# Bias products of a routed expert layer behind the expert loop, and nine expert weight loads issued by GpSimd two at a time

## The chip, the cores and the metric

One core of one Trainium2 chip. The metric is the device time of one execution in microseconds. TensorE is called PE, its weight loads PEld, VectorE DVE, ScalarE ACT, GpSimd POOL and SyncE SP, as in the profile. A "q" behind a name (SPq, ACTq) is that engine's sequencer, which issues DMAs.

## What is computed

`x` has 1250 rows of 512. It is normalized, goes through a graph layer (neighbour sums over 40,000 edges, then two matrix products with 1024 hidden columns) and an attention layer with 8 heads, and both results are added to `x`. The sum goes through a layer of 16 experts, of which each row uses two. Only this last part matters here:

```python
xt = layernorm(x)                                   # 1250 x 512
probs = softmax(xt @ router_w.T + router_b)         # 1250 x 16
topk_p, topk_i = top_k(probs, 2)
gates = sum(one_hot(topk_i) * topk_p[..., None], axis=1)      # 1250 x 16, two nonzero per row
for each expert e:
    h = gelu(xt @ w1[e].T + b1[e])                  # 256 hidden
    y = h @ w2[e].T + b2[e]                         # 512
    out += y * gates[:, e]
result = x + out
```

The sum over experts of gate times second bias is the product `gates @ b2` (1250 x 16 by 16 x 512), which the kernel computes by itself. It is called the bias product below.

## The kernel before

The 1250 rows are ten tiles of 128 (the last has 98). Each engine has its own program, and semaphores order them. The residual sum lies in SBUF as `xr`, tile by tile. An engine works through its program in order: an instruction behind a wait does not start before the wait is over.

**The graph layer's second half and the routing** run over the groups of tiles `FC_TILES` (0 to 2, 3 to 5, 6 and 7, 8 and 9). PE computes the hidden columns (L1234) and the second product (L1180), DVE adds it to `xr` (L948) and normalizes, PE turns the normalized rows and computes router logits (L1198), DVE picks the two best experts of each row, and PE counts how many earlier rows chose the same expert (L1205). DVE then knows for each row two slots in a DRAM buffer `slots`, sorted by expert (`place`). POOL scatters each tile's rows there, twice, with indirect DMAs (L552, 20 in all, semaphore `scattered`). After the last group DVE works out which expert each tile of slots belongs to and how many pairs of tiles there are, signals `route_ready` (L982), and computes the last gates (`weigh`, L983, semaphore `gates_ready`).

**The weights of the 16 experts** are 1 MB each (128 partitions of 8 KB, w1 and w2 together) and all fit in SBUF once the earlier parts are done. Each load is one DMA with a semaphore of its own, `ew_in[e]`. SP issues experts 0 and 15 (L376) while the graph layer runs, 9, 10 and 11 (L380) when its hidden columns are done, and 12, 13 and 14 (L391) just ahead of its part of the expert loop. ACT issues experts 1 to 8 (L668) when the graph layer's last product is done (`mix_ps`). POOL, after its last scatter, waits for the loads in the order of the experts and counts them into one semaphore, `w_ready` (L556 to L558), which DVE and PE compare with a number read at run time.

**The bias products** stand between routing and expert loop. For each tile PE turns its gates (L1265, into PSUM bank 0 or 1), ACT copies them out (L673, `gt_saved`), PE multiplies by `b2` (L1271, into bank 2 or 3), and DVE adds the result to `xr` (L988, `gb_added`). With two banks for each, PE's product of tile t waits for DVE's add of tile t - 2.

**The expert loop** takes two tiles of slots a turn. SP waits for `route_ready` and for all scatters, and fetches the first two tiles (L385, `xg_in`); PE turns them (`turn_rows`, L1277), ACT copies (L677), and SP fetches the next two (L388). DVE's `take_w1` (L994 to L998) waits for `w_ready` of the tile's expert and copies its w1 to a fixed place; PE's first product (L1295) needs that copy. ACT applies gelu (L687), PE turns the next rows and multiplies by w2 (L1308), DVE copies the result out (L1010), and SP stores it into `slots` (L400).

**The end.** When all results are stored, POOL gathers for each tile of rows the two results (L568, 20 indirect DMAs), DVE multiplies each by its gate and adds it to `xr` (L1015, L1017), and SP stores the tile (L405).

The order in which POOL counts, and what DVE waits for:

```python
for e in range(EXP):                      # POOL, L556
    pool.wait_ge(ew_in[e], 16)
    pool.sem_inc(w_ready, 1)
...
dve.wait_ge(w_ready, e + 1)               # DVE, take_w1, L997
dve.tensor_copy(w1_now[:, a, :], arena[:, bass.ds(lies, KD * DFF)]).then_inc(w1_ready[a], 1)
```

Of the kernel before, what the change touches and what calls it, by code (L numbers as in the profile page):

```python
# [23 lines left out]
P = 128  # L24
N = 1250
D = 512
NT = 10
# [6 lines left out]
FC_TILES = [range(0, 3), range(3, 6), range(6, 8), range(8, 10)]  # L34
# [18 lines left out]
EXP = 16  # L53
DFF = 256
KF = DFF // P
EW = KD * DFF + KF * D
# [10 lines left out]
def layer(nc, x, src, dst, wqkv, wo, bo, gw1, gb1, gw2, gb2, geps, rw, rb, ew, eb1, eb2, out):  # L67
    f32r = mybir.dt.float32r
    f32, f16, bf16, i32 = mybir.dt.float32, mybir.dt.float16, mybir.dt.bfloat16, mybir.dt.int32
    ALU = mybir.AluOpType  # L70
# [5 lines left out]
    with ExitStack() as ctx:  # L76
# [10 lines left out]
        arena = sb("arena", [P, SLAB // 4])  # L87
# [75 lines left out]
        xr = at(VT + NT * D * 4, [NT, D])  # L163
# [29 lines left out]
        ident = sb("ident", [P, P])  # L193
# [95 lines left out]
        def rows(t):  # L289
            return LAST if t == NT - 1 else P  # L290
# [45 lines left out]
        def _(sp):  # L336
# [25 lines left out]
            def expert(e):  # L362
                sp.dma_start(arena[:, expert_at(e):expert_at(e) + EW], ew[e]).then_inc(ew_in[e], 16)
# [23 lines left out]
                sp.wait_ge(xgt_ps[a], 1)  # L387
                sp.dma_start(xg[:, a, :], rows_of(2 + a)).then_inc(xg_in[a], 16)  # L388

            for e in (12, 13, 14):  # L390
                expert(e)  # L391
            n = sp.value_load(npair[0:1, 0:1], min_val=1, max_val=(MAXT - 3) // 2)
            with sp.Fori(0, n) as j:
                for a in range(2):
# [14 lines left out]
        def _(pool):  # L409
# [139 lines left out]
            for t in range(NT):  # L549
                pool.wait_ge(slots_ready, 1 + sum(1 for tiles in FC_TILES if tiles[-1] < t))  # L550
                for k in range(2):
                    pool.indirect_dma_start(  # L552
                        out=xs, out_offset=bass.IndirectOffsetOnAxis(ap=slot[0:rows(t), k, t:t + 1], axis=0),
                        in_=x2n[0:rows(t), t, :], in_offset=None).then_inc(scattered, 16)

            for e in range(EXP):  # L556
                pool.wait_ge(ew_in[e], 16)
                pool.sem_inc(w_ready, 1)  # L558
# [15 lines left out]
        def _(act):  # L574
# [89 lines left out]
                    act.activation(x2n_t[:, t % 2, :, :], bank[6][:, :].rearrange("p (k n) -> p k n", k=KD),  # L664
                                   copy).then_inc(x2nt_saved, 1)
            act.wait_ge(mix_ps, NT)
            for e in range(1, 9):
                act.dma_start(arena[:, expert_at(e):expert_at(e) + EW], ew[e]).then_inc(ew_in[e], 16)  # L668
            exponents(len(FC_TILES) - 1)

            for t in range(NT):
                act.wait_ge(gt_ps, t + 1)
                act.activation(gates_t[:, t * P:(t + 1) * P], bank[t % 2][0:EXP, 0:P], copy).then_inc(gt_saved, 1)  # L673

            for a in range(2):
                act.wait_ge(xgt_ps[a], 1)
                act.activation(xg_t[:, a, :, :], bank[4 + a][:, :].rearrange("p (k n) -> p k n", k=KD),  # L677
                               copy).then_inc(xgt_saved[a], 1)
            act.wait_ge(eb1_in, 16)
            act.wait_ge(route_ready, 1)  # L680
            n = act.value_load(npair[0:1, 0:1], min_val=1, max_val=(MAXT - 3) // 2)
# [15 lines left out]
        def _(dve):  # L697
# [284 lines left out]
            dve.sem_inc(route_ready, 1)  # L982
            weigh(len(FC_TILES) - 1)  # L983

            for t in range(NT):
                r = rows(t)
                dve.wait_ge(gb_ps, t + 1)
                dve.tensor_tensor(xr[0:r, t, :], xr[0:r, t, :], bank[2 + t % 2][0:r, :], ALU.add).then_inc(gb_added, 1)  # L988


            for a in range(2):
                dve.sem_inc(y_saved[a], 1)
                dve.sem_inc(y_stored[a], 16)
# [17 lines left out]

            for t in range(NT):
                r = rows(t)
                dve.wait_ge(yg_in[t], 32)
                link(dve.scalar_tensor_tensor(out=xr[0:r, t, :], in0=yg[0:r, 0, t, :], scalar=gate[0:r, 0, t:t + 1],  # L1015
                                              in1=xr[0:r, t, :], op0=ALU.mult, op1=ALU.add))
                dve.scalar_tensor_tensor(out=xr[0:r, t, :], in0=yg[0:r, 1, t, :], scalar=gate[0:r, 1, t:t + 1],  # L1017
                                         in1=xr[0:r, t, :], op0=ALU.mult, op1=ALU.add).then_inc(res_ready, 1)

        @block.tensor  # L1020
        def _(pe):
# [234 lines left out]
            route(NT - 1)  # L1256
            ranks(len(FC_TILES) - 1)

            pe.wait_ge(b2_in, 16)
            for f, tiles in enumerate(FC_TILES):  # L1260
                pe.wait_ge(gates_ready, f + 1)
                for t in tiles:
                    if t >= 2:
                        pe.wait_ge(gt_saved, t - 1)
                    pe.transpose(bank[t % 2][0:EXP, 0:P], gates[:, t, :], ident[:, :]).then_inc(gt_ps, 1)  # L1265
                for t in tiles:
                    r = rows(t)
                    pe.wait_ge(gt_saved, t + 1)
                    if t >= 2:
                        pe.wait_ge(gb_added, t - 1)  # L1270
                    pe.matmul(bank[2 + t % 2][0:r, :], gates_t[:, t * P:t * P + r], b2_sb[:, :],  # L1271
                              start=True, stop=True).then_inc(gb_ps, 1)


            def turn_rows(a):
                for k in range(KD):
                    ins = pe.transpose(bank[4 + a][:, k * P:(k + 1) * P], xg[:, a, k * P:(k + 1) * P], ident[:, :])  # L1277
                ins.then_inc(xgt_ps[a], 1)

            pe.wait_ge(x2_ready, NT)  # L1280
            for a in range(2):
                pe.wait_ge(xg_in[a], 16)
                turn_rows(a)
            pe.wait_ge(route_ready, 1)
            n = pe.value_load(npair[0:1, 0:1], min_val=1, max_val=(MAXT - 3) // 2)
            with pe.Fori(0, n) as j:
# [16 lines left out]
                for a in range(2):  # L1303
                    pe.wait_ge(w_ready, e[a] + 1)
                    pe.wait_ge(hg_ready[a], j + 1)
                    pe.wait_ge(y_saved[a], j + 1)
                    for k in range(KF):
                        ins = pe.matmul(bank[6 + a][:, :], hg_t[:, a, k, :],  # L1308
                                        arena[:, bass.ds(lies[a] + KD * DFF + k * D, D)],
                                        start=(k == 0), stop=(k == KF - 1))  # L1310
                    ins.then_inc(y_ps[a], 1)


# [29 lines left out]
```

## Time and profile before

| | |
|---|---|
| median of 3 runs | 882.88 us (881.28 to 884.25) |
| profiled execution, its own time | 883.28 us |
| its span in the profile | 881.5 us |
| mean granted PE clock | 0.942 |
| PE, DVE, ACT, POOL busy | 773.4, 519.3, 280.9, 154.5 us |

The span runs from the first to the last instruction of the profile. All positions below are microseconds from its start. Busy time of an engine counts neither waits nor the issuing of DMAs, except on POOL, whose DMA issues are listed as its work. The granted clock is a share of the full 2.4 GHz.

### The profile page before, as it was taken

How to read it: one execution, taken by the hardware profiler on the slowest of the kernel's cores; microseconds unless marked ns; L12 is line 12 of the kernel's file. 1: busy time of each engine (PE TensorE's matmuls, PEld its weight loads, DVE VectorE, ACT ScalarE, POOL GpSimd, SP SyncE). 2: the span in 40 equal slices, each digit the busy share in tenths (PEclk: the TensorE clock that was granted, in tenths of full speed). 3: DMA queues.
4: the chain of work that ended last, by engine and by line, in shares of the span. 5: the costliest groups of instructions: out<-in, count | busy, mean ns of one | idle time of the engine just before them, and what ended most of it. 6: DMA issues, size and time to landing. Idle time of an engine off the chain costs nothing.

```text
span 881.5 us, 11457 instructions
## 1 busy us (share of the span) xinstructions
PE 773.4 (88%) x3351; PEld 517.5 (59%) x3352; DVE 519.3 (59%) x1488; ACT 280.9 (32%) x575; POOL 154.5 (18%) x198
## 2 busy tenths in 40 slices
PE   1999998998989998989799999999998599999910
PEld 1555543665756665666577744677887256766700
DVE  6444345797989899888977535434445533333224
ACT  1311111352525443434345401323333123434400
POOL 5040002112040304040400043002021100000044
PEclk9999999998999999989899999999999559999965
DMA  9016000807153435344261081001015945343357
GB/s 301 2 41 242 1 0 1 293 2 237 59 165 131 140 145 160 134 124 172 65 230 48 1 336 67 1 0 63 10 73 191 365 183 197 108 139 111 129 167 229
DMA packets 47015, 111.61 MB, mean 127 GB/s; under 512 B 7034, under 2 KB 7050, under 8 KB 44528
## 3 DMA queue, kind: packets, MB, share of 16 engines
q1 hardware_dynamic: 42192, 91.41, 30.6%
q0 software_dynamic: 3616, 11.17, 4.0%
q10 hardware_dynamic: 1152, 8.39, 2.4%
q8 instruction: 24, 0.39, 0.2%
q14 instruction: 31, 0.25, 0.1%
HBM read 44.73 MB, written 58.54 MB: 117 GB/s over the span
## 4 chain that ended last, share of the span: by engine, by line
PE 72%; DVE 18%; issue 4%; POOL 2%; DMA 2%; ACT 1%; DVEq 0%; POOLq 0%; SPq 0%
PE bank L1082 9%; PE bank L1104 8%; PE bank L1234 7%; PE bank L1180 6%; PE bank L1295 6%; PE bank L1131 6%; PE bank L1308 5%; DVE arena L797 5%; DVE p_lo L833 5%; PE bank L1053 4%; PE bank L1114 4%; PE bank L1165 4%; PE bank L1150 4%; PE bank L1147 3%; DVE arena L799 3%
## 5 line engine op out<-in xcount | busy, mean ns | idle before, releaser
L630 ACT ACTIVATE p_hi<-bank 128x416 fp32r<-128x416 f32 (+1 forms) x240 | 124.0, 519 | 201.6 <-PE bank L1131 200.2
L833 DVE SCALAR_TENSOR_TENSOR p_lo<-bank,p_hi 128x416 fp32r<-128x416 f32 (+1 forms) x240 | 140.2, 586 | 40.8 <-ACT p_hi L630 39.7
L797 DVE TENSOR_SCALAR arena<-iota,arena 125x128 f16<-125x128 f16 x392 | 135.5, 346 | 42.0 <-PE bank L1053 39.8
L799 DVE TENSOR_SCALAR arena<-iota,arena 125x320 f16<-125x320 f16 x392 | 115.8, 295 | 0.0
L1131 PE MATMUL bank<-q_hi,k_hl 128*128 128x416 f32 (+1 forms) x240 | 114.6, 478 | 0.1
L1150 PE MATMUL bank<-p_lo,v_hl 128*128 128x416 f32 (+1 forms) x240 | 90.8, 378 | 22.4 <-DVE p_lo L833 22.0
L1082 PE MATMUL bank<-arena 128*128 128x512 f32 x200 | 103.9, 601 | 0.8 <-ACT arena L597 0.8
L1053 PE MATMUL bank<-arena 125*128 125x320 f16 x392 | 95.8, 309 | 5.1 <-issue 4.0
L1147 PE MATMUL bank<-p_hi,v_hl 128*128 128x416 f32 (+1 forms) x240 | 86.5, 360 | 0.0
L1131 PE MATMUL bank<-q_lo,k_hl 128*128 128x416 f32 (+1 forms) x240 | 86.1, 359 | 0.0
L1053 PEld LDWEIGHTS bank<-arena 125*128 125x128 f16 x392 | 34.4, 99 | 74.5 <-issue 53.8
L1104 PE MATMUL bank<-arena 128*128 128x416 f32 (+1 forms) x192 | 70.1, 513 | 0.8 <-ACT arena L582 0.8
L1234 PE MATMUL bank<-arena 128*128 128x384 f32 (+2 forms) x256 | 70.3, 430 | 0.0
L1150 PEld LDWEIGHTS bank<-p_lo,v_hl 128*128 128x128 f32 x240 | 46.4, 193 | 36.4 <-DVE p_lo L833 35.1
L1295 PEld LDWEIGHTS bank<-arena 128*128 128x128 f32 x448 | 52.8, 197 | 17.2 <-issue 15.8
L1295 PE MATMUL bank<-arena 128*128 128x128 f32 x448 | 55.1, 283 | 6.4 <-issue 5.4
L998 DVE COPY arena<-arena 128x1024 f32 x30 | 20.8, 695 | 66.9 <-issue 66.9
L1131 PEld LDWEIGHTS bank<-q_hi,k_hl 128*128 128x128 f32 x240 | 47.0, 196 | 20.2 <-issue 13.5
L1234 PEld LDWEIGHTS bank<-arena 128*128 128x128 f32 x256 | 47.7, 190 | 17.6 <-issue 0.5
L492 POOL COPY arena<-arena 125x20 f32 (+1 forms) x40 | 8.6, 214 | 249.7 <-DVE arena L799 213.7
L1104 PEld LDWEIGHTS bank<-arena 128*128 128x128 f32 x192 | 35.2, 189 | 27.1 <-issue 26.5
L1308 PE MATMUL bank<-arena 128*128 x112 | 50.4, 592 | 0.0
(208 smaller groups left out, 1019.4 us busy)
## 6 DMA issues: line engine op xcount, KB each, us to landing
slots<-arena SPq DMA_DIRECT2D x6, 5376.0 KB, 19.1
slots<-arena SPq DMA_DIRECT2D x2, 5120.0 KB, 19.1
arena<-in_ew SPq DMA_DIRECT2D x8, 1024.0 KB, 10.2
arena<-in_ew ACTq DMA_DIRECT2D x8, 1024.0 KB, 12.9
arena<-slots SPq DMA_DIRECT2D x32, 256.0 KB, 2.8
slots<-arena SPq DMA_DIRECT2D x28, 256.0 KB, 2.0
arena<-in_gw SPq DMA_DIRECT2D x2, 2048.0 KB, 17.0
arena<-in_wqkv SPq DMA_DIRECT2D x4, 768.0 KB, 16.5
```

Of the source, the lines that this page charges most:

```text
L630: act.activation(p_hi[0:kt, s % NPB, 0:n], bank[s % NQB][0:kt, 0:n], ACT.Relu).then_inc(p_hi_ready, 1)
L797: dve.tensor_scalar(ring[:, at_slot:at_slot + P], iota16[0:CE, 0:P], window_cols[:, i % WBUF, 1, k:k + 1], None, ALU.is_equal)
L799: dve.tensor_scalar(ring[:, at_slot + P:at_slot + OHW], iota16[0:CE, :], window_cols[:, i % WBUF, 0, k:k + 1], None, ALU.is_equal).then_in ...
L833: dve.scalar_tensor_tensor(out=p_lo[0:kt, s % NPB, 0:n], in0=bank[s % NQB][0:kt, 0:n], scalar=0.0, in1=p_hi[0:kt, s % NPB, 0:n].bitcast(f3 ...
L1053: return pe.matmul(bank[AW[w % 2]][:, 0:WCOL], of[:, at_slot:at_slot + P], of[:, at_slot + P:at_slot + OHW], start=start, stop=stop, skip_ ...
L1082: ins = pe.matmul(bank[NB][:, :], a_t[:, g % 2, t, :], xn[:, t, :], start=(t == 0), stop=(t == NT - 1))
L1104: ins = pe.matmul(bank[g % 5][:, 0:n], w_qkv[:, k, c:c + P], xn_t[:, k, o:o + n], start=(k == 0), stop=(k == KD - 1))
L1131: ins = pe.matmul(bank[s % NQB][0:kt, 0:n], k_hl[h % 2][:, t * P:t * P + kt], q[h % 2][:, o:o + n], start=first, stop=not first)
L1147: pe.matmul(bank[AV + m % 2][:, 0:n], v_hl[0:kt, t, h, :, :], p_hi[0:kt, s % NPB, 0:n], start=(t == 0), stop=False)
L1150: pe.matmul(bank[AV + m % 2][:, 0:n], v_hl[0:kt, t, h, :, :], p_lo[0:kt, s % NPB, 0:n], start=False, stop=(t == NT - 1)).then_inc(av_step, 1)
L1234: ins = pe.matmul(bank[g % 4][:, 0:n], w1[:, k, m * P:(m + 1) * P], rst_t[:, k, o:o + n], start=(k == 0), stop=(k == KD - 1))
L1295: ins = pe.matmul(bank[a][:, m * P:(m + 1) * P], w1_now[:, a, k * DFF + m * P:k * DFF + m * P + P], xg_t[:, a, k, :], start=(k == 0), stop ...
```

## The change

The bias products (PE L1271 and DVE's adds L988) move behind the expert loop; DVE's add for a tile stands ahead of that tile's two gate steps. The transposes of the gates stay ahead of the loop: the first three groups ahead of turning the first rows, the last group behind it; PE then waits until all are copied. Nine weight loads (experts 3 to 8, which ACT issued, and 12 to 14, which SP issued) are issued by POOL instead, after its last scatter and once `xg_in[1]` and `mix_ps` have come, each from the third on after the load two places before it has landed. They stand ahead of the loop that counts `w_ready`.

```diff
--- before.py
+++ after.py
@@ -387,8 +387,6 @@
                 sp.wait_ge(xgt_ps[a], 1)
                 sp.dma_start(xg[:, a, :], rows_of(2 + a)).then_inc(xg_in[a], 16)
 
-            for e in (12, 13, 14):
-                expert(e)
             n = sp.value_load(npair[0:1, 0:1], min_val=1, max_val=(MAXT - 3) // 2)
             with sp.Fori(0, n) as j:
                 for a in range(2):
@@ -553,6 +551,13 @@
                         out=xs, out_offset=bass.IndirectOffsetOnAxis(ap=slot[0:rows(t), k, t:t + 1], axis=0),
                         in_=x2n[0:rows(t), t, :], in_offset=None).then_inc(scattered, 16)
 
+            pool.wait_ge(xg_in[1], 16)
+            pool.wait_ge(mix_ps, NT)
+            late = (3, 4, 5, 6, 7, 8, 12, 13, 14)
+            for i, e in enumerate(late):
+                if i >= 2:
+                    pool.wait_ge(ew_in[late[i - 2]], 16)
+                pool.dma_start(arena[:, expert_at(e):expert_at(e) + EW], ew[e]).then_inc(ew_in[e], 16)
             for e in range(EXP):
                 pool.wait_ge(ew_in[e], 16)
                 pool.sem_inc(w_ready, 1)
@@ -664,18 +669,21 @@
                     act.activation(x2n_t[:, t % 2, :, :], bank[6][:, :].rearrange("p (k n) -> p k n", k=KD),
                                    copy).then_inc(x2nt_saved, 1)
             act.wait_ge(mix_ps, NT)
-            for e in range(1, 9):
+            for e in range(1, 3):
                 act.dma_start(arena[:, expert_at(e):expert_at(e) + EW], ew[e]).then_inc(ew_in[e], 16)
             exponents(len(FC_TILES) - 1)
 
-            for t in range(NT):
-                act.wait_ge(gt_ps, t + 1)
-                act.activation(gates_t[:, t * P:(t + 1) * P], bank[t % 2][0:EXP, 0:P], copy).then_inc(gt_saved, 1)
-
+            for tiles in FC_TILES[:-1]:
+                for t in tiles:
+                    act.wait_ge(gt_ps, t + 1)
+                    act.activation(gates_t[:, t * P:(t + 1) * P], bank[t % 2][0:EXP, 0:P], copy).then_inc(gt_saved, 1)
             for a in range(2):
                 act.wait_ge(xgt_ps[a], 1)
                 act.activation(xg_t[:, a, :, :], bank[4 + a][:, :].rearrange("p (k n) -> p k n", k=KD),
                                copy).then_inc(xgt_saved[a], 1)
+            for t in FC_TILES[-1]:
+                act.wait_ge(gt_ps, t + 1)
+                act.activation(gates_t[:, t * P:(t + 1) * P], bank[t % 2][0:EXP, 0:P], copy).then_inc(gt_saved, 1)
             act.wait_ge(eb1_in, 16)
             act.wait_ge(route_ready, 1)
             n = act.value_load(npair[0:1, 0:1], min_val=1, max_val=(MAXT - 3) // 2)
@@ -982,12 +990,6 @@
             dve.sem_inc(route_ready, 1)
             weigh(len(FC_TILES) - 1)
 
-            for t in range(NT):
-                r = rows(t)
-                dve.wait_ge(gb_ps, t + 1)
-                dve.tensor_tensor(xr[0:r, t, :], xr[0:r, t, :], bank[2 + t % 2][0:r, :], ALU.add).then_inc(gb_added, 1)
-
-
             for a in range(2):
                 dve.sem_inc(y_saved[a], 1)
                 dve.sem_inc(y_stored[a], 16)
@@ -1011,6 +1013,9 @@
 
             for t in range(NT):
                 r = rows(t)
+                dve.wait_ge(gb_ps, t + 1)
+                link(dve.tensor_tensor(xr[0:r, t, :], xr[0:r, t, :], bank[2 + t % 2][0:r, :], ALU.add))
+                dve.sem_inc(gb_added, 1)
                 dve.wait_ge(yg_in[t], 32)
                 link(dve.scalar_tensor_tensor(out=xr[0:r, t, :], in0=yg[0:r, 0, t, :], scalar=gate[0:r, 0, t:t + 1],
                                               in1=xr[0:r, t, :], op0=ALU.mult, op1=ALU.add))
@@ -1256,31 +1261,26 @@
             route(NT - 1)
             ranks(len(FC_TILES) - 1)
 
-            pe.wait_ge(b2_in, 16)
-            for f, tiles in enumerate(FC_TILES):
-                pe.wait_ge(gates_ready, f + 1)
-                for t in tiles:
-                    if t >= 2:
-                        pe.wait_ge(gt_saved, t - 1)
-                    pe.transpose(bank[t % 2][0:EXP, 0:P], gates[:, t, :], ident[:, :]).then_inc(gt_ps, 1)
-                for t in tiles:
-                    r = rows(t)
-                    pe.wait_ge(gt_saved, t + 1)
-                    if t >= 2:
-                        pe.wait_ge(gb_added, t - 1)
-                    pe.matmul(bank[2 + t % 2][0:r, :], gates_t[:, t * P:t * P + r], b2_sb[:, :],
-                              start=True, stop=True).then_inc(gb_ps, 1)
-
-
             def turn_rows(a):
                 for k in range(KD):
                     ins = pe.transpose(bank[4 + a][:, k * P:(k + 1) * P], xg[:, a, k * P:(k + 1) * P], ident[:, :])
                 ins.then_inc(xgt_ps[a], 1)
 
+            def turn_gates(f):
+                pe.wait_ge(gates_ready, f + 1)
+                for t in FC_TILES[f]:
+                    if t >= 2:
+                        pe.wait_ge(gt_saved, t - 1)
+                    pe.transpose(bank[t % 2][0:EXP, 0:P], gates[:, t, :], ident[:, :]).then_inc(gt_ps, 1)
+
+            for f in range(len(FC_TILES) - 1):
+                turn_gates(f)
             pe.wait_ge(x2_ready, NT)
             for a in range(2):
                 pe.wait_ge(xg_in[a], 16)
                 turn_rows(a)
+            turn_gates(len(FC_TILES) - 1)
+            pe.wait_ge(gt_saved, NT)
             pe.wait_ge(route_ready, 1)
             n = pe.value_load(npair[0:1, 0:1], min_val=1, max_val=(MAXT - 3) // 2)
             with pe.Fori(0, n) as j:
@@ -1310,6 +1310,14 @@
                                         start=(k == 0), stop=(k == KF - 1))
                     ins.then_inc(y_ps[a], 1)
 
+            pe.wait_ge(b2_in, 16)
+            for t in range(NT):
+                r = rows(t)
+                if t >= 2:
+                    pe.wait_ge(gb_added, t - 1)
+                pe.matmul(bank[2 + t % 2][0:r, :], gates_t[:, t * P:t * P + r], b2_sb[:, :],
+                          start=True, stop=True).then_inc(gb_ps, 1)
+
 
 # ---- launch: one core ----
 def kernel(x, src, dst, L0_gnn_W1, L0_gnn_b1, L0_gnn_W2, L0_gnn_b2, L0_gnn_eps, L0_mix_W_qkv, L0_mix_W_out,
```

## Rows read from the trace of the kernel before

**Rows 1.** Chain of waits: start us, us, what; biases and loop start

```profile
703.29 5.42 PE bank L1271 x6
...
719.76 0.70 DVE arena L998
720.51 5.55 PE bank L1295 x32
```

**Rows 2.** Timeline: start us, us, engine, line, op, out<-in, count [idle before <-releaser]

```profile
684.21 4.22 ACTq L668 DMA_DIRECT2D arena<-in_ew  x8
...
695.98 1.33 POOL L552 DMA_INDIRECT slots<-arena,slot  x1 [0.30 <-issue]
...
706.15 1.46 SPq L385 DMA_DIRECT2D arena<-slots  x2
...
717.53 1.97 PE L1277 MATMUL bank<-ident,arena 128*128 128x128 f32 x8
717.64 0.69 DVE L988 TENSOR_TENSOR arena<-arena,bank 98x512 f32<-98x512 f32 x1 [1.02 <-PE bank L1271]
...
721.31 1.70 SPq L363 DMA_DIRECT2D arena<-in_ew  x3
```

**Rows 3.** DMA rate, the stretch 678 to 730 in 40 slices of 1.3 us

```profile
GB/s 299 394 214 13 0 101 309 422 410 422 435 435 403 372 391 400 413 429 441 416 416 429 447 326 159 0 0 0 0 0 0 0 30 210 321 403 391 397 429 435
```

**Rows 4.** Weight loads: ACT's first, ACT's last two, SP's last two of 12 to 14

```profile
L668 ACTq DMA_DIRECT2D arena<-in_ew x1: 396/396/396, 684.2 to 684.2; - x1
DMA to landing us min/median/max: 5.1/5.1/5.1
...
L668 ACTq DMA_DIRECT2D arena<-in_ew x2: 473/475/477, 687.5 to 688.0; - x2
DMA to landing us min/median/max: 19.3/20.3/21.3
...
L363 SPq DMA_DIRECT2D arena<-in_ew x2: 445/593/741, 721.8 to 722.6; - x2
DMA to landing us min/median/max: 7.4/8.3/9.1
```

**Rows 5.** Windows: us, busy of each engine (count), PE clock, DMA share, GB/s

```profile
712.00:716.00 4.00, 3.86 (x7) 1.17 (x6) 0.93 (x3) 0.48 (x2) 0.00 (x0) 0.50 0.00 0
...
720.00:724.00 4.00, 3.49 (x16) 3.50 (x17) 1.15 (x2) 0.13 (x1) 0.00 (x0) 0.50 0.74 227
724.00:728.00 4.00, 4.00 (x29) 3.34 (x28) 0.99 (x2) 3.40 (x7) 0.00 (x0) 0.98 1.01 408
```

**Rows 6.** Chain of waits: second and third turn, last y copy, last gather

```profile
730.78 3.81 PE bank L1295 x32
...
739.31 3.81 PE bank L1295 x32
...
841.37 0.70 DVE arena L1010
...
871.81 5.45 DMA arena<-slots,slot
```

**Rows 7.** Timeline of the end: gathers on POOL, gate steps on DVE

```profile
847.37 0.96 POOL L568 DMA_INDIRECT arena<-slots,slot  x1 [0.30 <-issue]
...
850.89 0.75 DVE L1015 SCALAR_TENSOR_TENSOR arena<-arena,gate 128x512 f32<-128x512 f32 x1 [8.83 <-DMA arena<-slots,slot]
851.14 1.32 POOL L568 DMA_INDIRECT arena<-slots,slot  x1 [0.30 <-issue]
...
874.49 0.75 DVE L1017 SCALAR_TENSOR_TENSOR arena<-arena,gate 128x512 f32<-128x512 f32 x1
```

**Rows 8.** The page's DMA issues: count, KB each, median us to landing

```profile
arena<-slots SPq DMA_DIRECT2D x32, 256.0 KB, 2.8
slots<-arena SPq DMA_DIRECT2D x28, 256.0 KB, 2.0
```

**Rows 9.** Timeline: a plain DMA of 32 KB issued by POOL

```profile
6.59 0.52 POOL L428 DMA_DIRECT2D b_sb<-in_eb  x1
```

## The prediction

> **What bounds the kernel now.** I read the chain of waits first, for the stretch the edits touch. After the routing, PE and DVE alternate over the ten bias products: PE L1271 holds the chain in stretches such as the 5.42 us one at 703.29, the last add ends at 718.33, DVE copies the first expert's weights at 719.76, and the loop's first matmul starts at 720.51 [rows 1, 2]. The timeline then shows what stands beside that. ACT issued eight weight loads from 684.21; the last scatter left POOL at 695.98 + 1.33 = 697.31, yet SP, which waits for all scatters, could fetch the first rows only at 706.15 [rows 2], because the 16 DMA engines were full until 709: the rate line shows 372 to 447 GB/s in slice after slice [rows 3], and the last of ACT's loads, issued at 688.0, landed 21.3 us later, at 709.3 [rows 4]. From there to 719 the queues stand idle while PE works through the biases at the lower of its two clock levels [rows 3, 5]. So two delays overlap ahead of the loop: a full DMA side to 709 and the bias products to 718. Both are what the edits touch. The loop's first turn takes 10.27 us (720.51 to 730.78), the others 8.53 (739.31 - 730.78), 13 of them to the last y copy at 841.37 [rows 1, 6]; its instructions stay as they are. Behind it, POOL issues 20 gathers, and the end is set by the last gather and two DVE operations [rows 6, 7].
>
> **The change, part by part.** *Bias products leave the front.* The ten transposes of gates stay: eight are done while SP waits for the scatters, two after the rows are turned. PE's products, which alternate with DVE's adds up to 718.33, and those adds, ten of 0.69 us [rows 1, 2], go. By itself that would allow the loop to start when the rows are there.
>
> *When the first rows land.* Only experts 1 and 2 are now loaded by ACT. One load alone takes 5.1 us and each further one about 2.7 (below), so the engines are free by about 693, before the last scatter. That one still leaves POOL at 697.3. Its landing is not in the trace without competition: the plain 256 KB writes to the same tensor take 2.0 us in the median [rows 8], the last gather took 5.45 with its issue, some 4.5 without it (0.96), the second gather 850.89 - 848.33 = 2.56 [rows 6, 7]. I take 2.5, the gather in quiet queues, and get 699.8. SP's second row load starts 1.1 us after the first (both are issued within 1.46) [rows 2], at 701.0, and lands 2.8 later [rows 8]: **xg_in[1] at about 703.9**, where the kernel before could only issue it at 707.3. From turning the rows to the loop took 3.0 us before (717.53 to 720.51) [rows 1, 2]; with the last two gate transposes in between I take 3.6: PE could start the loop at 707.5.
>
> *The new wait.* POOL now issues nine loads, and stands still before the third and each later one until the load two places back has landed. Behind these, in POOL's program, comes the loop that signals w_ready for every expert, expert 0 included. DVE's take_w1 waits for w_ready, PE for w1_ready. Experts 0, 1 and 2 lie in SBUF long before, but nobody is told until the ninth load has been issued, and that needs the seventh one landed. So the loop's start is POOL's start plus seven loads, two in flight. Price of a load: 5.1 us for the first, from an idle queue; then the spacing of landings: ACT's eight are (709.3 - 689.3)/7 = 2.9 apart with scatters between them, SP's last two of experts 12 to 14 land at 721.8 + 7.4 = 729.2 and 722.6 + 9.1 = 731.7, 2.5 apart; I take 2.7 [rows 4]. That two in flight keep this pace is an estimate: one load's 5.1 us over two is 2.6, so they just do. To this come the next two row loads (0.5 MB, 1.2 us at 420 GB/s). Seventh landing: 5.1 + 6 x 2.7 + 1.2 = 22.5 us after POOL starts. No row shows POOL issuing a 1 MB load; a small plain one takes it 0.52 us, an indirect one 0.96 [rows 7, 9]. I take 0.6 for the ninth. Then 0.2 for the signal and 0.75 for the copy of w1 (719.76 to 720.51) [rows 1]. DVE's value loads are over by then. **First matmul: 704.0 + 22.5 + 0.6 + 0.2 + 0.75 = 728.1, against 720.5: 7.6 us later.**
>
> *Other waits.* SP loses three issues (1.70 us at 721.31 [rows 2]), which nobody waited for. PE idles some 20 us before the loop instead of working; the first turn was already run from the low clock (0.50 up to 724, 0.98 after) [rows 5], so I cost that at nothing; were the clock to come a turn later, it would cost up to the 1.7 us by which the first turn is longer now (10.27 - 8.53).
>
> *Bias products behind the loop.* PE has nothing to do there; its first two products need no wait. DVE gets ten adds of 0.69, with the wait behind each some 0.8, between tiles. POOL issues a pair of gathers per (871.81 - 847.37)/18 x 2 = 2.72 us, DVE now needs 1.53 per tile and would need 2.3 [rows 2, 6, 7]. They fit, and the cover is POOL's issuing. Where landings bunch, DVE falls behind: I follow it to the ninth tile done at about 876.0 instead of 875.24, the last add over at 876.8, and the last landing comes at 877.26 [rows 6, 7]. Half a microsecond is left; if it fails, one add, 0.8 us. POOL's gather issue beside a DVE operation took 1.32 instead of 0.96 [rows 7], so between 0 and 1 us could come on top. I take 0.3.
>
> *Sum.* +7.6 + 0.3 = +7.9 us. The profiled execution took 883.28 (span 881.5), the median is 882.88: 890.8.
>
> The Trainium skill, "DMA: Bandwidth & Descriptors", section on rules for kernel authors, speaks against this part of the change: issue a DMA early, compute, and wait for its semaphore late. Here the loads move from 684 to 704, into a stretch where everything waits for them; the idle queues between 693 and 704 would be the sign.
>
> **Rivals.** *A, on the other side: the signal does not bind, the loop starts with the rows.* Then the first matmul is at 707.5 and the kernel at 882.9 - 13.0 + 0.3 = 870.2. For it: the first experts lie there, and the DMA side is emptier when rows are fetched. Against it: POOL's program order. It decides where the seventh load lands before about 719 (720.5 less 1.55), 15 us after POOL's start: 7.34 MB in the 12 us after the first landing delay of some 3 us, that is over 600 GB/s, where the best slice shows 447 [rows 3]. 4%.
>
> *B, the loads run at the best rate seen.* 1.049 MB at 447 GB/s is 2.35 us a load; the scatter lands in 2.0, the two row loads cost nothing: 7.6 - 0.5 - 2.1 - 1.2 = +3.8, with the tail 887. For: full slices at 430 and over. Against: two in flight leave gaps that eight did not. 16%, a quarter of that within 0.3% of before. The Trainium skill, "DMA: Bandwidth & Descriptors", section on the anatomy of one DMA from GpSimd, gives an estimate of 2.0 us plus the bytes at 436 GB/s, 4.4 us alone and 2.4 for each further load: 18.8 us for seven, and about 887 too; no row here shows a 1 MB load from POOL.
>
> *C, POOL's loads do not keep the queue full.* After each landing POOL must wake and issue; if each issue adds to the pace instead of hiding, it is 2.7 + 0.7 (0.52 and a wake-up) to 2.7 + 0.96 us a load [rows 7, 9]: 6 x 0.7 = 4.2 to 5.8 more, 895 to 897. For: a single load's 5.1 us are twice what it takes from a full queue [rows 4]. 18%. Were nothing overlapped, 5.1 a load: 14.4 more, 905. 4%.
>
> *D, my case*, 888 to 894: 58%.
>
> **How the numbers follow.** A measurement of this kernel can tell about 0.3%, 2.6 us, from no change. Faster: A, 4%. Within: a quarter of B, 4%, and a little for the first loads landing sooner, 5% in all. Slower: 91%. The range takes in B less the spread of the runs (1.6 us), 885.5, and C with a late scatter (4.5 instead of 2.5), 898; left out are A, serial loads, and half of what is above C.
>
> **What would show it.** First L1295 near 728 and not 720.5, and the DVE copy L998 just ahead of it; POOL's nine issues from 704 on, the gaps between them 2.7; SP's first row load at about 700; DMA idle from 693 to 700; L1271 behind the loop; loop turns at 8.53; the stretch from the last y copy to the end as before, some 40 us, within 1. I am wrong if the first w1 copy stands before the ninth POOL load, or if the copies come after 735.

## The result and the profile after

The changed kernel takes **890.3 us** (median of 5 runs, 889.3 to 892.77), the kernel before, on the same chip, 882.69 (5 runs, 881.05 to 884.25): 7.6 us more, a ratio of 1.0095 with the 95% interval 1.0079 to 1.0111. The forecast was 890.8, and 7.9 more. The profiled execution took 890.1 us with a span of 888.1, against 883.28 and 881.5. In the code printed by the profile of the changed kernel the lines have moved: the transposes of the gates are L1274, turning the rows L1266, the bias product L1318, DVE's copy of w1 L1000, its bias add L1017, POOL's late loads L560 and its gathers L573. The loop's two products kept L1295 and L1308.

The chain of waits of the changed kernel ahead of the loop (start us, us, what). It answers to [rows 1] and to the first half of [rows 2]:

```profile
696.03 3.36 DMA slots<-arena,slot
...
700.42 0.34 SPq L385
...
701.55 2.81 DMA arena<-slots
704.36 0.29 issue
704.65 0.62 POOL arena L560
...
705.27 8.19 DMA arena<-in_ew
...
713.74 4.87 DMA arena<-in_ew
...
718.89 4.99 DMA arena<-in_ew
...
724.16 0.53 POOL arena L560
724.69 2.49 issue
727.18 0.02 POOLq L563
...
727.33 0.70 DVE arena L1000
728.03 0.04 issue
728.08 5.29 PE bank L1295 x32
```

Read it downwards. The last scatter, the row load and then the second, fourth and sixth weight load, one behind another, carry the chain; no PE or DVE work stands in it between the routing and 727.33. PE's first product starts at 728.08, where before it started at 720.51. The "issue" of 2.49 us at 724.69 is POOL standing at its wait for the seventh load.

The timeline of POOL's loads and of the engines that wait (start us, us, engine line op, idle before and what ended it):

```profile
704.65 1.20 POOL L560 DMA_DIRECT2D arena<-in_ew  x2 [7.29 <-DMA arena<-slots]
...
710.68 0.53 POOL L560 DMA_DIRECT2D arena<-in_ew  x1 [4.84 <-DMA arena<-in_ew]
713.74 0.53 POOL L560 DMA_DIRECT2D arena<-in_ew  x1 [2.53 <-DMA arena<-in_ew]
...
727.19 0.95 POOL L560 DMA_DIRECT2D arena<-in_ew  x1 [2.50 <-DMA arena<-in_ew]
727.33 0.69 DVE L1000 COPY arena<-arena 128x1024 f32 x1 [28.07 <-POOLq L563]
```

DVE sat 28 us in front of the copy, and what released it is POOL's sequencer at L563, the line that counts `w_ready`. The copy began 0.14 us after the recorded start of the ninth load's issue, at 727.19. This is the row on which the result hangs: the weights of experts 1 and 2, which ACT issues at 684, had landed by 692, and in e1, whose signal comes early, DVE makes this copy at 700.54.

Two windows (us, busy of PE, PEld, DVE, ACT, POOL with counts, PE clock, DMA share, GB/s), to lay beside [rows 5]:

```profile
692.00:696.00 4.00, 1.17 (x4) 0.27 (x3) 3.76 (x12) 1.16 (x5) 3.05 (x3) 0.50 0.34 131
...
716.00:720.00 4.00, 0.00 (x0) 0.00 (x0) 0.00 (x0) 0.00 (x0) 1.05 (x2) 0.50 1.00 399
```

The queues now idle for two thirds where they used to be full, and are full where they used to be idle; in the second window nothing but the DMA engines and POOL's issuing is at work.

From the loop on little differs. The chain shows the second turn at 738.10, the third at 746.64 (8.54 us a turn, as in [rows 6]) and the last y copy at 848.54; the first turn takes 10.02 us against 10.27. Of the 6.6 us by which the span grew, 7.57 arose ahead of the loop, -0.25 in the first turn, -0.15 in the other thirteen (841.37 - 730.78 against 848.54 - 738.10), and the rest, some -0.6, from the last copy on.

### The profile page after: what moved, and what is told of

It reads as the page before. It is cut to its first block, busy times and chain, and to the rows that moved or that the text cites. A ratio compares the mean times of both kernels' runs of the same rounds, so it can differ in the third digit from the quotient of the medians.

```text
span 888.1 us, 11460 instructions
## 1 busy us (share of the span) xinstructions
PE 773.9 (87%) x3351; PEld 517.0 (58%) x3352; DVE 517.4 (58%) x1488; ACT 280.4 (32%) x575; POOL 160.1 (18%) x207
## 4 chain that ended last, share of the span: by engine, by line
PE 67%; DVE 18%; issue 6%; DMA 5%; POOL 3%; ACT 1%; SPq 0%; POOLq 0%; DVEq 0%
PE bank L1087 8%; PE bank L1109 8%; PE bank L1239 7%; PE bank L1295 6%; DVE arena L805 6%; PE bank L1136 6%; DVE p_lo L841 5%; PE bank L1308 5%; PE bank L1185 5%; PE bank L1058 4%; PE bank L1119 4%; PE bank L1170 4%; DVE arena L807 3%; PE bank L1155 3%; PE bank L1152 3%
## 5 line engine op out<-in xcount | busy, mean ns | idle before, releaser
L1295 PE MATMUL bank<-arena 128*128 128x128 f32 x448 | 54.8, 282 | 27.4 <-DVE arena L1000 22.1
L1000 DVE COPY arena<-arena 128x1024 f32 x30 | 20.8, 694 | 93.3 <-issue 60.7
L1295 PEld LDWEIGHTS bank<-arena 128*128 128x128 f32 x448 | 52.5, 196 | 38.3 <-DVE arena L1000 22.6
L1308 PE MATMUL bank<-arena 128*128 x112 | 50.4, 592 | 0.0
```

The source lines that it names most:

```text
L1295: ins = pe.matmul(bank[a][:, m * P:(m + 1) * P], w1_now[:, a, k * DFF + m * P:k * DFF + m * P + P], xg_t[:, a, k, :], start=(k == 0), stop ...
```

## Experiments

Each kernel was timed against the kernel before on the same chip. "After" is the changed kernel. The kernel before took 882.69 us on the chip of the result, 881.51 on that of e1 to e4, 882.56 on that of e5 to e8 and 882.29 on that of f1 to f4; so kernels of different groups are compared by their ratios.

| kernel | median us | ratio to before, 95% interval | loop start | turns 1, 2, 3 |
|---|---|---|---|---|
| before | 882.69 | 1 | 720.51 | 10.27, 8.53, 8.65 |
| after | 890.30 | 1.0095 (1.0079 to 1.0111) | 728.08 | 10.02, 8.54, 8.51 |
| e3 loads only | 891.50 | 1.0115 (1.0098 to 1.0132) | 727.94 | 11.28, 8.52, 8.65 |
| e2 biases only | 878.61 | 0.9961 (0.9947 to 0.9975) | 716.73 | 10.27, 8.55, 8.53 |
| e4 early signal, biases in front | 883.10 | 1.0015 (1.0004 to 1.0026) | 720.50 | 10.28, 12.08, 8.43 |
| e1 early signal | 876.62 | 0.9928 (0.9907 to 0.9949) | 709.59 | 10.16, 8.57, 13.30 |
| e5 one in flight | 912.17 | 1.0332 (1.0306 to 1.0359) | 749.57 | 10.97, 8.53, 8.50 |
| e6 four in flight | 884.78 | 1.0024 (1.0009 to 1.0039) | 721.29 | 11.03, 8.53, 8.49 |
| e7 nine in flight | 877.31 | 0.9936 (0.9911 to 0.9961) | 712.09 | 10.25, 12.80, 8.46 |
| e8 adds first | 873.93 | 0.9892 (0.9866 to 0.9917) | 710.41 | 10.10, 8.53, 8.73 |
| f1 gates wait later | 870.46 | 0.9859 (0.9839 to 0.9880) | 708.33 | 10.97, 8.55, 8.64 |
| f2 one in flight | 872.36 | 0.9891 (0.9875 to 0.9907) | 707.52 | 10.89, 10.53, 8.50 |
| f3 all three | 872.25 | 0.9883 (0.9865 to 0.9901) | 707.61 | 11.13, 10.90, 8.50 |
| f4 biases only, gates wait later | 877.46 | 0.9950 (0.9934 to 0.9967) | 712.55 | 11.36, 8.53, 8.49 |

Loop start and turns are from one profiled execution each; a turn is the distance between the first matmuls of two turns. e8 has one more long turn, its fourth, of 12.38. These turns come from single executions, and not always typical ones: the profiled executions of e4 (886.36 us), e8 (876.15) and f3 (874.69) were the slowest of their kernels, 2.2 to 3.3 us above the median, and each of them has a turn of 10.9 to 12.4 us behind its first. A long turn of these three may be missing in their other executions.

The positions carry a shift of their own, too: POOL starts its late loads anywhere between 703.58 us (e6) and 706.24 (e7), though the changed kernel, e5, e6 and e7 do not differ ahead of that. A difference of a microsecond or two between two loop starts has to be read with that in mind.

### Which part costs: e1 to e4

**e1_signal_early.** POOL counts a load as soon as it has waited for it. `tell(n)` waits for and counts all experts below n that have not been counted yet (its definition and the issuing line are left out here):

```diff
...
+            tell(3)
             pool.wait_ge(xg_in[1], 16)
...
                 if i >= 2:
                     pool.wait_ge(ew_in[late[i - 2]], 16)
+                    tell(late[i - 2] + 1)
...
-            for e in range(EXP):
-                pool.wait_ge(ew_in[e], 16)
-                pool.sem_inc(w_ready, 1)
+            tell(EXP)
```

> The changed kernel, but POOL counts an expert into w_ready as soon as it knows its load has landed: 0, 1 and 2 before the first late load, 3 to 8 between the late loads, the rest behind. Same loads, same two in flight. Theory S (the late signal alone holds the loop): the first w1 copy and the first L1295 matmul stand near 707.5 us instead of 728.1, and the kernel takes 870 to 872 us. Theory T (moving 9 MB at that point holds the loop, through the DMA queues or the row loads): the loop starts well after 707.5 or its first turns stretch, and the kernel stays above 880.

The loads, their number in flight and their place are unchanged, and the loop starts 18.5 us sooner, at 709.59. That settles the late signal as what held it. But 876.6 us is not 870 to 872. Two things stand in its chain of waits that the expectation did not have (start us, us, what):

```profile
705.42 0.17 ACT arena L694
705.59 4.00 issue
709.59 2.47 PE bank L1303 x10
...
726.07 9.88 DMA arena<-slots
```

PE waits 4.00 us for nothing that the profile shows, between the last gates copy and the first product, and a row load of 256 KB that is issued at 726.07 takes 9.88 us, which makes the third turn 13.30 us long. The first is taken up by f1 and f4, the second by e7 and f2.

**e2_biases_only.** The diff of the change without its DMA parts: ACT issues 1 to 8, SP 12 to 14.

> Only the bias products move; the weight loads stay with ACT (1 to 8) and SP (12 to 14) as in the kernel before. Theory S: the bias products did hold the loop, but behind them stand the rows, late from the full queues; the first rows land near 710.7 us, the loop starts near 714, and the kernel takes 876 to 877 us. If the bias products were no cost (or their place behind the loop costs as much), 882 to 883.

876 to 877 was too hopeful by some 2 us: the ratio is clearly below 1, the rows land as expected (the second row load at 710.5), but the loop starts at 716.73 and not at 714, because the same gap, here 4.01 us, stands ahead of it. Without the bias products in front the loop starts 3.8 us sooner, and the medians on that chip differ by 2.9.

**e3_loads_only.** The change's DMA parts alone, bias products in front.

> Only the loads move to POOL, two in flight, ahead of the counting loop; the bias products stay in front. Theory S: the first rows land near 704, the ninth load goes out near 727, the loop starts near 728 all the same, the kernel takes 889.5 to 891.5 us, so the whole loss belongs to this part. If PE's idle time ahead of the loop costs something by itself (the clock), this one, which has PE busy to 718, is faster than the changed kernel by 1 us or more in the first turn.

891.5 us and a loop start of 727.94: the whole loss is this part's. PE was busy to 718 here and idle in the changed kernel, yet the first turn is longer here, 11.28 against 10.02. So these two executions show no cost of PE's idling ahead of the loop; the forecast had it at nothing.

**e4_signal_early_biases_front.** e1's signal, the bias products where the kernel before has them.

> The early signal of e1_signal_early with the bias products left in front of the loop. Theory S: the bias products are the last thing ahead of the loop again, it starts at 719.5 to 720.5 us and the kernel takes 881.5 to 883 us: neither part gains without the other. Theory that the loads' timing alone brings a gain: below 880.

883.1 us, at the upper edge of what was expected, and loop start 720.50, the same as before to a hundredth. With e1, e2 and e3 this makes a square: late loads with a late signal lose 1.0 to 1.2% wherever the biases are, late loads with an early signal gain nothing while the biases stand in front, and moving the biases gains 0.4% alone but 0.9% on top of late loads with an early signal (0.9928 against 1.0015). Neither part pays by itself as much as both, once the signal is early.

### How much in flight: e5 to e7

The only edit is the distance in POOL's wait, or its absence:

```diff
-                if i >= 2:
-                    pool.wait_ge(ew_in[late[i - 2]], 16)
+                if i >= 1:
+                    pool.wait_ge(ew_in[late[i - 1]], 16)
```

This is e5's; e6 has `i >= 4` and `late[i - 4]`, and in e7 both lines are gone.

> The changed kernel with one late load in flight instead of two: each waits for the one before it. Theory S: the ninth issue needs the eighth landing, each load 4.9 to 5.4 us by itself plus 0.3 to wake; ninth issue near 704.7 + 43 = 748 us, loop start near 749, the kernel takes 909 to 913 us. If the loop's start hung on something else than POOL's position, it would stay near 890.

> The changed kernel with four late loads in flight. Theory S: the ninth issue needs the fifth landing; by the pace of two in flight that is 16 to 16.7 us after 704.7, so the loop starts near 722 us and the kernel takes 883 to 885 us. A pace that gets clearly better than 2.7 us a load with four in flight would show two in flight as a brake of its own, and give 881 to 883.

> The changed kernel with no wait between the nine late loads; the counting loop still stands behind them. Theory S: POOL is through in nine issues of 0.55 to 0.95 us, the signals come near 710.5, the loop starts near 711 us, and the kernel takes 873 to 875 us, even though all 9 MB compete at once. Theory T (the traffic itself hurts the loop): the rows of the first turns land late, turns of over 10 us, kernel above 878.

The loop starts at 749.57, 728.08, 721.29 and 712.09 us with one, two, four and nine in flight; expected were 749, (728.1), 722 and 711. From POOL's first late issue to the loop's start it is 44.8, 23.4, 17.7 and 5.9 us. With one, two and four in flight POOL's last issue sets the start. With nine something else does, as e7's chain of waits shows (start us, us, what):

```profile
709.93 0.70 DVE arena L998
710.63 1.46 issue
712.09 5.52 PE bank L1293 x32
```

The copy of w1 is over at 710.63, but PE starts only 1.46 us later. That is 4.04 us after ACT's last gates copy (over at 708.05), the same stretch as in e1; f1 and f4 tell what it is. The timeline of e5's POOL shows the price of a load alone:

```profile
704.78 0.62 POOL L560 DMA_DIRECT2D arena<-in_ew  x1 [7.50 <-DMA arena<-slots]
710.69 0.56 POOL L560 DMA_DIRECT2D arena<-in_ew  x1 [5.29 <-DMA arena<-in_ew]
716.01 0.53 POOL L560 DMA_DIRECT2D arena<-in_ew  x1 [4.76 <-DMA arena<-in_ew]
...
748.68 0.95 POOL L560 DMA_DIRECT2D arena<-in_ew  x1 [4.75 <-DMA arena<-in_ew]
```

5.43 us from issue to issue on average ((748.68 - 710.69)/7), against (727.19 - 710.68)/6 = 2.75 with two in flight. In e6, from the fifth issue at 709.75 to the ninth at 720.41, it is 2.67: two in flight were no brake on the rate. e6 and e7 also show that the traffic can hurt: e7's loop starts 16.0 us sooner than the changed kernel's, but its ratio is only 0.0159 lower, some 14 us. Its 877.3 us lie between what theory S expected (873 to 875) and theory T (above 878): a row load issued at 720.1 takes 9.61 us and makes the second turn 12.80. Theory T is not the cause of the loss, but it takes its share of the gain.

### The two remainders: e8, f1 to f4

**e8_adds_first.** e1 with DVE's ten adds in a loop of their own ahead of the first wait for gathered rows.

> e1_signal_early with all ten of DVE's bias adds ahead of its first wait for gathered rows, where DVE waits some 8 us anyway, instead of one ahead of each tile. Theory: the add ahead of the last tile costs up to one add, 0.7 us, at the end, so this is 0 to 0.8 us faster than e1_signal_early, and the stretch from the last y copy to the last gate step is 36 us or a little less; if the adds were hidden between the tiles, no difference; if ten adds with PE in turn take longer than the wait, it is slower by up to 1.5 us.

The adds run in the gap, from 836.04 on, and are over at 849.01; the last tile's two gate steps then start at its landing, 869.96. From the last y copy's start to the end of the last gate step it takes 36.51 us, in e1 37.18, in the changed kernel 36.81 and in the kernel before 37.45. The other kernels scatter as widely: with all bias products in front of the loop e3 has 36.40 and e4 36.96, with them behind it e2 has 36.36 and e7 35.99. By its median e8 is some 3 us faster than e1, more than the 0.8 that the theory allows, but the intervals of the two overlap, and f3 against f2 shows no difference. The place of the adds is worth less than these runs resolve.

**f1_gates_wait_later.** PE need not know that the gates are copied until it overwrites banks 0 and 1:

```diff
-            pe.wait_ge(gt_saved, NT)
             pe.wait_ge(route_ready, 1)
             n = pe.value_load(npair[0:1, 0:1], min_val=1, max_val=(MAXT - 3) // 2)
             with pe.Fori(0, n) as j:
...
+                pe.wait_ge(gt_saved, NT)
                 for a in range(2):
                     pe.wait_ge(w1_ready[a], j + 1)
```

> e1_signal_early with PE's wait for the last copied gates moved from ahead of its value loads to behind them, inside the loop (always met after the first turn). In e1_signal_early PE stood 4.0 us between that copy and its first L1295. Theory V (PE's sequencer starts its value loads only after that wait, and they take the 4 us): the loop starts 2.5 to 4 us sooner, at 705.5 to 707, and the kernel gains as much, 873 to 874 us. Theory F (the 4 us belong to full DMA queues, from which PE's program is fetched): no change, start at 709.6, 876 to 877 us.

**f4_biases_only_gates_wait_later.** The same edit on e2.

> e2_biases_only with the same wait moved behind the value loads; ACT and SP load the weights. There PE stood 4.0 us between the last gates copy at 712.7 and L1290 at 716.7. Theory V: the loop starts at 712.8 to 714, the kernel takes 875 to 876 us. Theory F (full queues): no change, since the queues were idle there anyway from 709 on; a gain here with a gain in f1 speaks for V, no gain in both for a fixed cost of entering the loop.

The chains of waits of f1 and then of f4 (start us, us, what):

```profile
701.17 3.00 DMA arena<-slots
...
706.28 2.06 issue
708.33 6.26 PE bank L1303 x32
```

```profile
710.79 1.76 issue
712.55 6.64 PE bank L1290 x32
```

f1's loop starts later than theory V expected (708.33 against 705.5 to 707), and yet the kernel is faster than expected, 870.5 us against 873 to 874; f4 starts at 712.55, just ahead of its 712.8 to 714. The stretch behind the last gates copy falls from 4.00 to 2.06 and from 4.01 to 1.76 us, not by the whole 4. The rest needs no second cause. Once PE's wait for the copies stands behind its value loads, the last wait ahead of them is the one for the second row load, and that comes only some two microseconds sooner. In f1 it lands at 704.17 and the first product starts 4.16 us later; in f4 it is issued at 705.2, lands at 708.4, and the first product follows 4.15 us later; in f2 and f3 it is 4.16 and 4.17. In e1, e2, e7 and e8 the last wait is the one for the gates copies, and the first product starts 4.00, 4.01, 4.04 and 4.04 us behind it. So in eight kernels PE needs 4.0 to 4.2 us from the last wait ahead of its value loads to the first product, and theory V covers the whole gap; what it had wrong is how much sooner that last wait can end. In the stretch PE's program has five value loads and the entry of the loop, and the profile shows no work in it; how the 4 us divide among them stays open. Theory F, full queues, does not fit: the DMA side moved 423 GB/s in the short gap of f1 and 275 in the long one of e2 (so it was not idle there, as f4's expectation had it). In the kernel before the gap did not show: there DVE's copy of w1 was the last to end.

f1 is the fastest of all, 0.9859; of its distance to e1 (0.9928) only 1.3 us is a sooner start (its second row load landed 0.7 us later than e1's), and the rest is that the profiled execution of f1 has no turn above 8.83 after the first, where that of e1 has one of 13.30. That is no accident of one execution: f1's four took 868.03 to 871.34 us, e1's four 873.56 to 877.03. Why the row loads beside POOL's weight loads took at most 6.2 us in f1's loop and 9.9 in e1's, with two in flight in both, these runs don't tell, and the two kernels ran on different chips. f4 was expected at 875 to 876 us and took 877.46; its interval overlaps that of e2, so the sooner start is shown by the trace and not by the time.

f4 gives part of its start back. It begins 4.18 us sooner than e2, of which 2.1 were there before the edit could act (its second row load landed at 708.4, that of e2 at 710.5), and has its second turn only 3.09 sooner (723.91 against 727.00). Windows of f4, then of the changed kernel (columns as above):

```profile
714.00:716.00 2.00, 2.00 (x11) 2.00 (x11) 0.00 (x0) 0.00 (x0) 0.00 (x0) 0.50 1.04 418
716.00:718.00 2.00, 2.00 (x11) 2.00 (x11) 0.04 (x1) 1.56 (x3) 0.00 (x0) 0.50 0.98 389
718.00:720.00 2.00, 2.00 (x18) 2.00 (x17) 0.65 (x1) 1.02 (x5) 0.00 (x0) 0.88 1.02 410
```

```profile
728.00:730.00 2.00, 1.92 (x9) 1.92 (x10) 0.72 (x2) 0.00 (x0) 0.14 (x1) 0.50 0.90 242
730.00:732.00 2.00, 2.00 (x15) 2.00 (x15) 0.00 (x0) 0.29 (x1) 0.00 (x0) 0.71 1.00 422
```

f4's PE works from 712.55 at 0.50, the 1.2 GHz level, until 718, and does 11 matmuls in 2 us; the changed kernel is at a mean of 0.71 in the window from 1.9 us after its start on. The first 32 products take 6.64 us in the one and 5.29 in the other.

**f2_one_in_flight and f3_all_three.** f1 with `i >= 1` and `late[i - 1]`, and that with e8's edit.

> f1_gates_wait_later with one late load in flight instead of two; the signals stay early. Theory R (in e1_signal_early and e7_nine_in_flight the row loads of the third turn took 9.9 us because they share the queues with weight loads, and cost one turn 5 us): with one in flight they land in under 7 us, no turn but the first is over 9 us, and the kernel gains 3 to 5 us on f1, to 869 to 871 us. If even one load in flight delays rows as much, the stretched turn stays and nothing is gained; if the experts come too late at 5.3 us each, turns stretch at DVE's copy of w1.

> f2_one_in_flight with all ten bias adds ahead of DVE's first wait for gathered rows, as in e8_adds_first. From e1 and e8 the add behind the ninth tile is worth 0 to 0.7 us: 868.5 to 871 us, not slower than f2. Loop start, turns as in f2.

Theory R fell. f2 is 872.4, no faster than f1 (870.5) and above the 869 to 871 that were expected; f3, with 872.3, is above its 868.5 to 871 and no different from f2. The chain of f2 has the long row load in the second turn:

```profile
715.48 0.27 SPq L366
...
716.18 8.16 DMA arena<-slots
724.39 0.66 PE bank L1274 x4
```

A single weight load in flight, beside the loop's own stores of 256 KB, is enough for 8.16 us, and POOL's loads spread over 50 us then, so more turns are exposed to them. The experts did not come too late: no turn is held by DVE's copy. f3's third and later turns hold one more long one, its fifth, of 10.19.

## Why the prediction was right

*The sum.* Forecast +7.6 at the loop's start and +0.3 behind the loop. Measured in the profiled pair: +7.57 at the start, -0.4 in the turns and -0.6 behind, and +7.6 between the medians. The mechanism is the one forecast, and the one large term carries the result.

*The bound of the kernel before.* That two delays lay over one another ahead of the loop, full queues and bias products, is shown by the square of e1 to e4. Taking away either one moves the start little: e2 by 3.8 us, e4 by nothing.

*The first rows.* Forecast: second row load landed at 703.9. Measured: scatter landed at 699.4, second row load issued at 701.5 and landed at 704.36. The landing of the scatter, the term with the widest bounds (2.0 to 4.5 us), was about 2.0 behind its issue (3.36 - 1.33), the lower end and not the 2.5 taken; what SP does between that landing and its first row load took 1.04 us (699.38 to 700.42, a value load of 0.48 in it), for which the sum had 0.1. POOL's wake-up, 0.29, was not in it either. So POOL was 0.65 late, at 704.65.

*The new wait.* This is the step that carries the result. Forecast: seventh landing 22.5 us after POOL's start, by 5.1 for the first and 2.7 for each further load plus 1.2 for two row loads. Measured: the seventh load landed at 726.9, 22.3 us after POOL's start, and the ninth was issued at 22.54 (727.19 - 704.65). The parts were less exact than the sum: the first load landed after 5.8 us and the second after 8.2, beside the row loads, and the pace behind was 2.75. That POOL's program order makes `w_ready` wait for all this is shown by e1, which changes only the signal and starts the loop at 709.59, and by e5 and e6, which change only the distance.

*The signal and the copy.* Forecast 0.6 for the ninth issue, 0.2 and 0.75. Measured 0.14 from the start of that issue to DVE's copy, and 0.75. POOL's sequencer counted at 727.18, while the issue of the ninth load is recorded from 727.19 to 728.14. That is 0.66 us less than in the sum and happens to cancel POOL's late start: 728.08 against 728.1. The agreement to a hundredth is luck, that within a microsecond is not.

*PE's idling, costed at nothing.* Nothing speaks against it: the first turn was 0.25 us shorter, though first turns scatter by 1.3 us over all the kernels.

*The bias products behind the loop, costed at 0.3.* The stretch from the last y copy on was some 0.6 us shorter: DVE finished 5.4 us after POOL's last gather issue (885.35 - 879.93) and before 5.9 (878.82 - 872.91). The half microsecond of slack that the forecast counted was gone: in the changed kernel the last two tiles run on DVE without a pause (start us, us, what, from the chain of waits):

```profile
881.53 0.76 DVE arena L1020
...
882.32 0.75 DVE arena L1022
883.07 0.60 DVE arena L1017
...
883.82 0.76 DVE arena L1020
...
884.60 0.75 DVE arena L1022
```

The add L1017 stands in the chain that ends the kernel. It costs at most its 0.7 us, and e8 and f3 don't resolve it. Nor do these traces resolve the 0.3 of the forecast or the 0.6 measured against it: over the kernels this stretch scatters from 35.99 to 37.45 us.

*The rivals.* A, the loop starting with the rows, did not come about. Its 707.5 was too early besides: it took 3.6 us from the second row load to the first product and had no term for PE's value loads, where f1 shows 4.16 from that landing and e1 6.11 (703.48 to 709.59), because its last wait comes later. B, the best rate: the loads ran at 399 GB/s in the window shown, not 447. The Trainium skill, "DMA: Bandwidth & Descriptors", section on the anatomy of one DMA from GpSimd, gives 2.0 us plus the bytes at 436 GB/s. By an estimate from it such a load takes 4.4 us alone and 2.4 more behind another. The traces disagree: in e5, with one in flight, it is 5.43 us from issue to issue, of which some 0.3 is POOL's wake-up, and in the changed kernel 2.75. The measurement decides. C, a brake of the issuing on the pace, is excluded by e6, whose pace with four in flight is the same within 0.1 us.

## What to carry to other kernels

A semaphore that counts arrivals in order is only as early as the engine that counts: before a wait is put ahead of such a loop, list what stands behind it in the same program and who waits for that. With the bias products moved and the same spacing of the loads, the kernel lost 1.0% with the signal behind them and gained 0.7% with the signal between, and 1.4% after one more unneeded wait was taken from ahead of PE's value loads. No run shows that the spacing itself gains anything: nine loads at once with the late signal gave 0.6%. A wait that an engine needs only before it overwrites a buffer belongs behind its value loads, not in front of them: PE had 4.0 to 4.2 us between the last wait ahead of its value loads and its first product, and moving one wait brought 2.

## What was not expected of the hardware

A 256 KB row load issued by SP took 5.0 and 4.4 us beside three weight loads from SP in the kernel before. Beside weight loads from POOL it varied far more: 3.8 and 3.2 in one turn of e1 and 7.8 and 9.9 in the next, 3.9 and then 8.6 in one turn of e4 (two in flight in both), up to 9.6 with nine (e7) and 8.2 with one (f2). The number in flight does not order these. Rows of f2, SP's first and second load of one turn, each with its time to landing:

```profile
L395 SPq DMA_DIRECT2D arena<-slots x1: 336/336/336, 715.0 to 715.0; - x1
DMA to landing us min/median/max: 2.7/2.7/2.7
...
L395 SPq DMA_DIRECT2D arena<-slots x1: 332/332/332, 716.2 to 716.2; - x1
DMA to landing us min/median/max: 8.2/8.2/8.2
```

POOL's next load was issued at 715.65, between the two. The order of issue is no rule, though: e4's load of 8.64 us was issued at 728.55, 0.5 us ahead of POOL's next one, at 729.05, and 3.7 behind the one before. The Trainium skill, "DMA: Bandwidth & Descriptors", section on issuing engines, says that DMAs of all issuers run on the same 16 engines and interleave; the delays agree with that in kind, but with what share each is served, and why 256 KB wait so much longer in one case than in another, stays open. Nor was it expected that the clock's rise would be so uneven: the first turn took between 10.02 and 11.36 us in these kernels, the shortest after 22 us of an idle PE, and 10.97 after 42 us of it (e5).
